# A graph network's last stage: dense-weight groups built two in a row, and tiles that cover 40 places instead of 48

## What is computed

```python
# N=3125 nodes, 128 features; E=103125 edges sorted by dst; 3 GCN layers, then one relational layer
norm = (dinv[src] * dinv[dst])[:, None]
for l in range(3):
    hw = h @ conv_w[l].T
    h  = elu(segment_sum(hw[src] * norm, dst) + conv_b[l]) + h
x = layernorm(x + concat(h_list) @ lin_w.T + lin_b)
# relational layer: 8 relations, each a mix of 4 bases
W   = einsum('rb,bio->rio', w_comp, bases)
agg = segment_sum(x[src] * edge_weight[:, None], edge_type * N + dst)     # [8, N, 128]
x = layernorm(x + einsum('rni,rio->no', agg, W))
```

## Time and profile before

| what | us |
|---|---|
| median of 3 runs (1128.03 to 1134.76) | 1131.08 |
| the profiled execution | 1125.61 |
| its span, first to last instruction | 1123.7 |
| PE busy in the span | 1028.7 |
| DVE busy | 816.6 |
| POOL busy | 508.9 |
| ACT busy | 443.5 |

### The profile page before, as it was taken

One profiled execution on the slowest core, in us unless ns is written; L12 is line 12 of the kernel. 1 busy time (PEld: TensorE's weight loads), 2 busy tenths in 40 slices (PEclk: granted clock), 3 DMA queues, 4 the chain that ended last, 5 costly groups with the idle time before them and its releaser, 6 DMA issues.

```text
span 1123.7 us, 23482 instructions
## 1 busy us (share of the span) xinstructions
PE 1028.7 (92%) x9508; PEld 680.6 (61%) x9508; DVE 816.6 (73%) x1702; ACT 443.5 (39%) x1027; POOL 508.9 (45%) x542
## 2 busy tenths in 40 slices
PE   1578889989999999995799999999999999999997
PEld 1575556656644564464666666666666666666665
DVE  4789899997546556888867777677777667677753
ACT  1598889887200040015423323233233233233320
POOL 5053000000077400000777777677776776776772
PEclk9877999999999999998699999999999999999999
DMA  5253000000111010101422222222222222222221
GB/s 159 51 190 92 1 1 1 1 1 1 58 25 27 8 58 1 44 15 54 118 53 56 58 57 51 55 53 55 55 53 53 57 50 55 55 53 54 58 51 32
DMA packets 48801, 55.34 MB, mean 49 GB/s; under 512 B 15543, under 2 KB 39129, under 8 KB 48182
## 3 DMA queue, kind: packets, MB, share of 16 engines
q0 software_dynamic: 16240, 31.95, 11.4%
q1 hardware_dynamic: 32454, 21.87, 6.8%
HBM read 42.10 MB, written 8.49 MB: 45 GB/s over the span
## 4 chain that ended last, share of the span: by engine, by line
PE 74%; DVE 14%; issue 5%; SPq 2%; ACT 2%; DMA 2%; DVEq 1%; POOL 0%
PE ps L1684 22%; PE ps L1537 20%; PE ps L1663 16%; PE ps L1678 11%; DVE arena L1107 8%; SPq L681 2%; PE ps L1526 1%; PE ps L1691 1%; PE ps L1697 1%; DMA dinv_col<-dinv_scratch 1%; DVE arena L1259 1%; PE ps L1514 1%; DMA arena<-in_dst_dram 1%; PE ps L1484 1%; DVE work L1118 1%
## 5 line engine op out<-in xcount | busy, mean ns | idle before, releaser
L837 POOL DMA_INDIRECT arena<-x_scratch,arena x437 | 412.4, 944 | 185.6 <-issue 110.2
L1537 PE MATMUL ps<-arena,u 125*128 125x480 fp8e5 (+1 forms) x1575 | 358.5, 354 | 1.2 <-ACT arena L891 1.2
L972 ACT COPY arena<-ps 125x400 f32<-125x400 f32 x364 | 169.9, 526 | 375.1 <-PE ps L1678 332.6
L1684 PE MATMUL ps<-arena,u 125*128 125x448 f32 x650 | 297.8, 539 | 0.0
L1663 PE MATMUL ps<-hT,arena 128*128 128x192 f32 x874 | 223.4, 348 | 1.4
L1537 PEld LDWEIGHTS ps<-arena,u 125*128 125x128 bf16 x1575 | 152.5, 97 | 108.1 <-ACT arena L891 1.7
L1663 PEld LDWEIGHTS ps<-hT,arena 128*128 128x128 f32 x874 | 147.4, 190 | 86.0 <-issue 73.3
L1107 DVE TENSOR_TENSOR arena<-arena 128x2048 bf16<-128x2048 bf16 (+2 forms) x158 | 188.8, 1254 | 12.7 <-PE ps L1526 9.5
L1526 PE MATMUL ps<-arena 128*128 128x125 bf16 x1256 | 148.3, 231 | 31.8 <-DVE arena L1107 29.8
L1678 PEld LDWEIGHTS ps<-dinv_all,u 64*128 64x128 bf16 x4368 | 108.8, 96 | 106.3 <-issue 85.6
L1330 DVE TENSOR_TENSOR u<-ps,arena 128x512 bf16<-128x512 bf16 x182 | 76.4, 420 | 111.7 <-PE ps L1678 90.7
(11 more groups left out here) (187 smaller groups left out, 705.9 us busy)
## 6 DMA issues: line engine op xcount, KB each, us to landing
arena<-x_scratch,arena POOLq DMA_INDIRECT x437, 2.5
arena<-hT SPq DMA_DIRECT2D x2, 1562.5 KB, 7.1
edge_scratch<-arena SPq DMA_DIRECT2D x5, 403.0 KB, 5.2
arena<-in_x_dram SPq DMA_DIRECT2D x1, 1562.5 KB
dinv_all<-dinv_scratch SPq DMA_DIRECT2D x1, 1562.5 KB, 8.8
h_scratch<-hT SPq DMA_DIRECT2D x1, 1562.5 KB, 6.8
first_term_scratch<-arena SPq DMA_DIRECT2D x1, 1562.5 KB
arena<-first_term_scratch SPq DMA_DIRECT2D x1, 1562.5 KB
```

The costliest lines, as they stand in the source:

```text
L837: nc.gpsimd.indirect_dma_start(out=gat[:, j, :], out_offset=None, in_=x1_d, in_offset=bass.IndirectOffsetOnAxis(ap=idxg[:, j:j + 1], axis= ...
L972: nc.scalar.copy(o, ps[0:BLK, octet_bank(k, w), 0:4 * ND].rearrange("p (i m) -> p m i", i=4)).then_inc(s_se, 1)
L1537: return T.matmul(ps[:, agg_bank(l, c), 0:CW[c]], u[0:BLK, s, k, :], region[:, s, 0:CW[c]], start=(first and s == 0 and k == 0), stop=(end ...
L1684: last = T.matmul(ps[:, 5, 0:NB * DN].rearrange("p (b n) -> p b n", b=NB), xb[0:BLK, s, :], sD[half][0:BLK].rearrange("p (b v) n -> p b v ...
```

## The change

Four things are changed together. (1) `WN` 48 to 40 and `WBACK` 21 to 18: a tile's matmul has 160 columns, not 192, and DVE's operand for it too. (2) `octet(k)` and `octet(k+1)` stand one behind the other, on PE and on DVE, behind tiles 4, 9, 14, 18, 23, 28 and at the chunk's start (before: singly, behind tiles 2, 4, 7, 9, 11, 14, 16, 18, 21, 23, 25, 28, 30 and at the start); the two use banks (2,3) and (6,7), and PE waits for the evictions of group k-2, not for half of k-1's. (3) `finish_dense` moves from tile 18 to tile 10 and into bank 5, `finish` from tile 24 to tile 15 and into the end of bank 0. Bank 5 is also where `dense` adds, so the wait for `s_dv` (`stats_dense` has read bank 5) now stands ahead of the first `dense` of a half, behind tile 15. (4) `HB` 7 to 4: bank 1 takes over from tile 12; on DVE `stats_dense` moves from batch 8 to 6, `ahead_of` from 8 to 7, `stats` and `lower` from 9 to 8.

```diff
-    KR = QA - (-23 * QD // TPB)
+    KR = QA - (-16 * QD // TPB)
-    WN = 48
-    WBACK = 21
+    WN = 40
+    WBACK = 18
-    HB = 7
+    HB = 4
-        OCTET_BANKS = ((6, 7), (2, 6), (7, 2))
+        OCTET_BANKS = ((2, 3), (6, 7))
 # DVE, chunk()
                         if q == 0:
                             octet(c, QA)
+                            octet(c, QA + 1)
                         moving(c, q, rank == 0)
...
-                        for k in range(QA + 1, end):
+                        if q == 7 and rank >= 1:
+                            ahead_of(c, HB)
+                        for k in range(QA + 2, end, 2):
                             if STEP.index(k - QA) - 1 in range(BT * q, BT * q + BT):
-                                prepare(c, k)
-                                octet(c, k)
-                        if q == 8 and rank >= 1:
-                            ahead_of(c, HB)
+                                for m in (k, k + 1):
+                                    prepare(c, m)
+                                    octet(c, m)
+                        if q == 6 and rank >= 1:
...
                             stats_dense(c - 1)
...
-                        if q == 9:
+                        if q == 8:
 # PE, octet()
-                    if k >= 1:
-                        pe.wait_ge(s_se, c * (2 * QD) + 2 * k - 1)
+                    if k >= 2:
+                        pe.wait_ge(s_se, c * (2 * QD) + 2 * (k - 1))
 # PE, chunk()
                         if j == DJ:
                             pe.wait_ge(s_se, c * (2 * QD) + 2 * QD)
+                            if rank >= 1:
+                                pe.wait_ge(s_dv, c)
                         if j >= DJ:
                             dense(j - DJ, half)
                         if rank >= 1:
-                            if j == 18:
-                                if rank >= 2:
-                                    pe.wait_ge(s_fv, c - 1)
+                            if j == 10:
                                 finish_dense(c - 1)
-                            if j == 24:
+                            if j == 15:
                                 pe.wait_ge(s_af, c)
-                                pe.wait_ge(s_dv, c)
                                 finish(c - 1)
                         k = QA + STEP[j + 1]
-                        if STEP[j] < STEP[j + 1] < QD and k < end:
+                        if STEP[j] < STEP[j + 1] < QD and STEP[j + 1] % 2 == 0 and k < end:
                             octet(c, k)
+                            octet(c, k + 1)
```

More of the change, by code:

```diff
@@ L57, in build_program @@
     KC = QA - (-DLEFT * QD // TPB)
-    KR = QA - (-23 * QD // TPB)
+    KR = QA - (-16 * QD // TPB)
     NP3 = 3 * NB
     ND = NB * NBLK
-    assert NCHK == DH + 1 and DN == 8 * QD and KC < QD <= KR < QA + QD - 1 and PG <= 6
+    assert NCHK == DH + 1 and DN == 8 * QD and KC < QD <= KR < QA + QD - 1 and PG <= 6 and QA % 2 == 0 and QD % 2 == 0
     PADN = 4095
@@ L92, in build_program @@
     ABOVE = P - WBACK
-    SPLIT = (P * BT) * 7 // TPB - WBACK
-    HB = 7
+    SPLIT = (P * BT) * 4 // TPB - WBACK
+    LW = P * (4 * BT - 1) // TPB + WN
+    HB = 4
     SPILL = LO[TPB - 1] + WN - P
@@ L242, in build_program, with turned @@
         aggD = work[:, 2, 0:NB * DN].rearrange("p (b n) -> p b n", b=NB)
-        accN = [ps[:, k, 0:NB * P].rearrange("p (b n) -> p b n", b=NB) for k in range(3)]
+        accN = [ps[:, k, 0:NB * w].rearrange("p (b n) -> p b n", b=NB) for k, w in enumerate((LW, P, P))]
+        assert LO[HB * BT] >= SPLIT and P - SPLIT + SPILL <= P and NB * LW + D <= 512
+        def turned(bank):
+            return ps[:, bank, 512 - D:512] if bank == 0 else ps[:, bank, 0:D]
         bnst = carve(A_BN, UBT * 8, fp32, 4).rearrange("p (t s) -> p t s", t=UBT)
@@ L267, in build_program @@
         maskP = uall[:, 2 * NBLK * D + 1024:2 * NBLK * D + 1024 + 4 * QD * NBLK].rearrange("p (g v t) -> p g v t", v=NBLK, t=2)
-        OCTET_BANKS = ((6, 7), (2, 6), (7, 2))
+        OCTET_BANKS = ((2, 3), (6, 7))
         def octet_bank(k, w):
-            return (6, 2)[w] if k % QD == QD - 1 else OCTET_BANKS[k % QD % 3][w]
+            return OCTET_BANKS[k % 2][w]
         MS = 4
@@ L1339, in lower @@
                 def lower(c):
-                    V.memset(aggf[:, :, ABOVE:P], 0.0)
-                    V.tensor_tensor(aggf[:, :, 0:ABOVE], accN[0][:, :, AT:P], carry[:, :, 0:ABOVE], ALU.add).then_inc(s_low, 1)
+                    V.memset(aggf[:, :, LW - AT:P], 0.0)
+                    V.tensor_tensor(aggf[:, :, 0:LW - AT], accN[0][:, :, AT:LW], carry[:, :, 0:LW - AT], ALU.add).then_inc(s_low, 1)
                     dve.wait_ge(s_low, c + 1)
@@ L1364, in stats, with stats_dense @@
                     V.bn_aggr(fst[:, 6:8], fst[:, 0:6]).then_inc(s_fv, 1)
-                def stats_dense(h, bank=3):
+                def stats_dense(h, bank=5):
                     dve.wait_ge(s_df, h + 1)
                     yv = ystageD[0:DN, 1, :]
-                    link(V.tensor_tensor(yv, ps[0:DN, bank, 0:D], x1rD[0:DN, ds(h, 1), :].rearrange("p s d -> p (s d)"), ALU.add))
+                    link(V.tensor_tensor(yv, turned(bank)[0:DN], x1rD[0:DN, ds(h, 1), :].rearrange("p s d -> p (s d)"), ALU.add))
                     link(V.bn_stats(fstD[0:DN, 0:6], yv))
@@ L1452, in _ @@
                 stats_dense(DH - 1, 6)
-                stats(C - 1)
+                stats(C - 1, 3)
                 norm_dense(DH - 1, False)
@@ L1687, in dense, with finish, finish_dense @@
                         last.then_inc(s_dp, 1)
-                def finish(c, bank=3):
+                def finish(c, bank=0):
                     for b in range(NB):
-                        last = T.matmul(ps[:, bank, 0:D], aggf[:, b, :], basesS[:, b, :], start=(b == 0), stop=(b == NB - 1))
+                        last = T.matmul(turned(bank), aggf[:, b, :], basesS[:, b, :], start=(b == 0), stop=(b == NB - 1))
                     last.then_inc(s_fin, 1)
-                def finish_dense(h, bank=3):
+                def finish_dense(h, bank=5):
                     pe.wait_ge(s_da, h + 1)
                     for b in range(NB):
-                        last = T.matmul(ps[0:DN, bank, 0:D], aggD[:, b, :], basesS[:, b, :], start=(b == 0), stop=(b == NB - 1))
+                        last = T.matmul(turned(bank)[0:DN], aggD[:, b, :], basesS[:, b, :], start=(b == 0), stop=(b == NB - 1))
                     last.then_inc(s_df, 1)
@@ L1756, in _ @@
                         pe.wait_ge(s_dv, DH - 1)
-                        finish(C - 1)
+                        finish(C - 1, 3)
                 pe.wait_ge(s_af, C + 1)
```

4 lines of the change are left out of this document (2 added, 2 removed).

## The result

| | before | changed |
|---|---|---|
| median of 4 runs each, us | 1131.66 | 1116.35 |
| lowest to highest, us | 1128.03 to 1134.76 | 1115.27 to 1118.01 |
| profiled execution, its span, us | 1125.61, 1123.7 | 1115.95, 1114.2 |
| mean granted clock | 0.965 | 0.956 |
| stage, first group to the span's end, us | 588.5 | 573.0 |

The ratio is 0.987, 95% interval 0.984 to 0.990: faster, by 15.3 us of the median. The forecast was 1122 (1104 to 1135).

What follows compares the result with a forecast made beforehand. PE's own instruction list was taken as the bound, POOL's gathers next. Gains of 9.4 + 5.7 + 2.8 = 18 us, less 8.5 for clock falls, gave 9.5 us off the 1131.08 median: 1122 us, range 1104 to 1135.

Steps and rivals of the forecast that it cites:

- Narrower tiles: PE's tile matmuls at 160 columns: 0.055 us less a tile, 1.8 us a chunk, 24 us over 437 tiles.
- Pairs: Groups back to back on PE: seven switches of 0.19 saved in each full chunk, 1.35 us.
- The moved transforms: Behind tile 15 PE waits 2.0 us for `s_dv`, then 0.3 for `s_af`: 2.3 us in each of chunks 1 to 11.
- Chunks: Length of a chunk in the stage: 42.8 us without a fall of the clock, 44.5 with one.
- The clock: Behind the new wait PE's clock falls in 5 of 11 chunks, 1.7 us each: 8.5 us lost, bounds 0 and 19.
- Start and chunk 0: Stage start without waits for ACT, plus chunk 0's shorter list: chunk 1 begins at 583.1 instead of 588.83, 5.7 us gained.
- The end: Chunk 12 and the rest: 41 narrower tiles and three saved switches, 2.8 us gained.
- The sum: Whole stage: 18 us gained without the clock, less 8.5 for its falls, 9.5 us less.
- The second: Rival: no wait worth naming behind tile 15, POOL's gathers become the bound; span ends at 1095, 1102 us; chance 0.10.
- The first: Rival: the wait behind tile 15 comes but the clock stays at 2.4 GHz; 18 us gained, 1113 us; chance 0.17.
- The third: Rival: each wait takes the clock down, no change at 1132, or slower where waits are longer, up to 1143; chance 0.25.
- The fourth: Rival: weight loads bind PE's tiles, so narrowing gives nothing; 24 us less gain, 1137 us; chance 0.03.

Runs made afterwards that it cites:

- the second execution: The changed kernel itself measured again with nothing altered, on a chip where the kernel before takes 1131.0 us: 1115.0 us, ratio 0.986.
- the fills: Changed kernel plus eight matmuls of zeros on PE where it waits for the statistics: 1108.0 us, ratio 0.979; on two other chips 1.060 and 1.059.

## Why the prediction was right, point by point

- **Narrower tiles.** 0.055 us a tile, 1.8 a chunk, as the kernel with that part alone shows once DVE's wait of 0.2 is taken off. Right. The upper bound of "0.065 (in proportion to the width)" was a slip: a sixth of 0.327 is 0.055, the same as the price taken.
- **Pairs.** Mis-sized: "Seven switches of 0.19 go in each full chunk: 1.35 us" is 1.97. The second group costs 0.55 and not 0.66, which no row of before could show; why is open. The bounds of 0 and 0.19 for a switch were too low, since they counted switches only.
- **The moved transforms.** "PE waits 2.0 us": 2.08 in nine of eleven chunks; before the first two (0.58 and 1.59) PE has waited for a gather, so the sum is 2.0 there too. `finish` was to wait 0.3 more and takes 0.14 more: it starts 0.89 behind its product where the clock stays up (650.14 to 651.03 in chunk 2), where a product alone is 0.75. The fixed sum of both is 2.2, predicted 2.3.
- **Chunks.** 42.8 and 44.5 predicted, 42.10 and 43.7 measured; of the 0.7 between, 0.6 is the pairs' term and 0.1 the waits'.
- **The clock.** Five falls of 1.7 us predicted, six of 1.65, seven in the second execution. That the waits bring it down and what a fall costs was right, and is shown by the fills. The number was a choice between 0 and 11 with two waits to go by; that it came so near is luck.
- **Start and chunk 0.** 5.7 predicted, 5.2 measured. The groups come every 1.2 us as worked out. **The end:** 2.8, measured 3.0.
- **The sum.** 9.5 us of the stage were forecast, 15.45 came. Chunks 1 to 11 hold the difference: they gave 7.3 us in place of 9.4 - 8.5 = 0.9. The pairs gave 11 x 0.62 = 6.8 more, `finish` 11 x 0.16 = 1.8 more, the shorter first waits 1.1 more; the sixth fall took 1.4, and two waits for a gather that I hadn't seen took 1.9. That is 6.4. "Its counterpart takes about 1116" came out at 1115.95 by luck: the stage was 6 us better than forecast, and its first group stood 6 us later in that execution. The median, some 6 us below the forecast of 1122, shows the miss.
- **Rivals.** The second (the gathers become the bound) is not what happened, but it is what lies behind: without the wait the kernel takes 1098, forecast 1102, and its span is 1095.6, forecast 1095. The first (the wait without falls) is the kernel with the fills: 1108, forecast 1113. The third (a fall behind each wait, or a longer wait) did not come: six and seven falls of eleven, and no wait over 2.1. The fourth (tiles bound by their weight load) is ruled out by the tile at 0.28 from start to start, with the same 128x128 load, and by the 21 us of the narrower tile alone.

The versions on the chips where before takes 1131, medians in us, and in brackets the stage in the trace, from its first group to the span's end:

| | one group at a time | pairs, statistics behind groups 8 and 9 | pairs, statistics first |
|---|---|---|---|
| 48 places | 1131 (588.5) | 1136 (592.9) | 1103 (561.2) |
| 40 places | 1110 (566.9) | 1116 (573.0) | 1098 (559.8) |

The narrower tile is worth 20 to 21 us until the gathers bound the chunk, then 1 (stage) to 5 (medians). The pairs, with the new banks and the moved transforms, are worth 28 us at 48 places, and their wait with its clock falls costs 33: the change as it was made is the narrower tile, less 6 us. Those three parts were never run apart, but the rows give the pairs 14 x (0.655 + 0.19) - 7 x (1.21 + 0.19) = 2.0 us of a chunk, which is the measured 1.97. Best is the version with pairs, 40 places and statistics first, 1098: 2.8% below before.

## What to carry to other kernels

When work is moved ahead on the engine that bounds the kernel, write down where on the other engine's list its input now stands, and move that ahead too: the same pairs that gained nothing behind a wait gained 28 us with one block of DVE's list put two groups earlier. A wait of 2 us in each iteration costs more than its length, since the clock may fall behind it (1.65 us each time here); work of no use in the wait gave that back on one kind of chip, but on the other that kernel was 6% slower than before, and taking the wait away gained 10 us more than filling it (1098 against 1108). And measure each part of a change alone: the whole was faster only by the part that was two constants.

## What the runs showed of the hardware that I had not expected

- Two chips on which one and the same kernel took 1312 instead of 1131 us. The signal of a finished group came 2.7 us late in the case above, and PE stood idle by itself. The two edits tried there that gain 2% elsewhere (the narrower tile; pairs at 48 places with the statistics first) gained nothing, and the statistics first gained 1 to 1.6% in place of 2.8.
- A second group of 24 small matmuls right behind the first costs 0.55 us, 0.11 less than one that stands alone (0.66), and the 0.19 of switching is saved besides.
- The clock fell behind six of nine waits of 2.08 us in each of two executions, and in the second once behind two waits of 1.08 and 0.94 with a tile between.
- In unchanged code the first group of the stage comes at one of two times: 535.2, 535.8 and 536.5 us in three profiled executions, 541.2 to 543.5 in five. From 200 to 300 us the changed kernel's clock is at 0.95 (first row), that of the version with the statistics first, which started early, at 0.98 (second). Nothing in either edit reaches that stretch, and what sets the clock apart there is open:

```profile
200.00:300.00 100.00, 90.80 (x793) 0.95 0.05 13
```

```profile
200.00:300.00 100.00, 93.08 (x813) 0.98 0.06 17
```

  Such a shift of 6 us, made ahead of the edited code, is more than several of the terms above; only differences within the stage are free of it.
